# First stage of a gated attention and expert kernel: written-out orders, and the next stage's first weights and key rows loaded in it

## What is computed

```python
ek = jnp.exp(jnp.minimum(kf, 30.0)); ekv = ek * vf          # keys = values = the side input
a = a * decay + ekv_t; b = b * decay + ek_t                 # forward (nf, df), backward (nb, db)
euk = jnp.exp(jnp.minimum(u + kf, 30.0))
num = nf + nb - ekv + euk * vf
den = df + db - ek + euk
base = jax.nn.sigmoid(r) * (num / jnp.maximum(den, 1e-08))
...
q = (x @ Wq + bq).reshape(b, h, t, dh)
k = (x @ Wk + bk).reshape(b, t, h, dh).transpose(0, 2, 3, 1)
v = (x @ Wv + bv).reshape(b, t, h, dh).transpose(0, 2, 1, 3)
logits = jnp.einsum('bhtd,bhds->bhts', q, k) * scale
weights = jax.nn.softmax(logits + mask, axis=-1)
return out @ Wo + bo
```

## Time and profile before

| | us |
|---|---|
| runs of the kernel | 2507.57 median of 3 (2503.07 to 2509.45) |
| the profiled execution | 2524.23, its span 2522.4 |
| PE busy | 2255.8 (89%) |
| GpSimd busy | 1442.2 (57%) |
| VectorE busy | 1264.3 (50%) |
| ScalarE busy | 1165.6 (46%) |
| mean granted clock of TensorE | 0.95 of full |

### The profile page before, as it was taken

How to read it: one execution, slowest core, us unless ns; L and a number is a source line. 1 busy time by engine, 2 the same in 40 slices (tenths; PEclk the granted TensorE clock), 3 DMA queues, 4 the chain that set the end, 5 groups by cost and what they waited for, 6 DMA issues and landing times. The chain is left out here.

```text
span 2522.4 us, 42005 instructions
## 1 busy us (share of the span) xinstructions
PE 2255.8 (89%) x12059; PEld 1931.3 (77%) x12060; DVE 1264.3 (50%) x2118; ACT 1165.6 (46%) x2503; POOL 1442.2 (57%) x980
## 2 busy tenths in 40 slices
PE   1579999999999999898887989999999799999776
PEld 1458888888888878777776779999998699999654
DVE  6737777777765666757642322222222122222365
ACT  3347777777777767775621123333322133333210
POOL 7747777777755466565723036250659966430376
PEclk6789999999999999999978999999999899999887
DMA  4243444433364445443357045343547655442376
GB/s 121 71 131 113 126 126 131 159 120 114 116 214 126 145 160 178 158 162 133 134 200 276 5 133 181 112 156 98 182 147 221 199 186 179 148 164 77 117 205 179
DMA packets 285670, 372.37 MB, mean 148 GB/s; under 512 B 20212, under 2 KB 187192, under 8 KB 280824
## 3 DMA queue, kind: packets, MB, share of 16 engines
q1 hardware_dynamic: 229112, 251.41, 31.7%
q10 hardware_dynamic: 41088, 69.22, 8.3%
q0 software_dynamic: 15360, 50.34, 6.1%
HBM read 257.66 MB, written 113.25 MB: 147 GB/s over the span
## 5 line engine op out<-in xcount | busy, mean ns | idle before, releaser
L1933 POOL TENSOR_SCALAR we_high<-we_raw 128x1408 fp32r<-128x1408 f32 (+1 forms) x95 | 133.9, 1410 | 414.4 <-PE up_e L649 314.9
L1935 POOL TENSOR_TENSOR we_low<-we_raw,we_high 128x1408 fp32r<-128x1408 f32 (+1 forms) x95 | 314.6, 3311 | 7.9
L2064 DVE TENSOR_TENSOR hT_low<-hT_ps,hT_high 128x256 fp32r<-128x256 f32 x127 | 54.0, 425 | 391.4 <-ACT hT_high L2027 391.4
L2077 DVE TENSOR_TENSOR hidden_e<-silu_e,up_e 128x352 f32<-128x352 f32 x127 | 66.2, 521 | 282.6 <-ACT silu_e L2038 282.6
L2038 ACT ACTIVATE silu_e<-gate_e 128x352 f32<-128x352 f32 x127 | 59.0, 465 | 315.9 <-PE up_e L649 315.9
L649 PE MATMUL gate_e<-we_high,xT_high 128*128 x508 | 177.4, 349 | 21.1 <-POOL we_low L1935 20.7
L2043 ACT ACTIVATE rows_out<-down_e 128x512 f32<-128x512 f32 x127 | 75.9, 598 | 216.5 <-PE down_e L649 216.5
L649 PE MATMUL gate_e<-we_high,xT_low 128*128 x508 | 165.5, 326 | 0.0
L649 PE MATMUL gate_e<-we_low,xT_high 128*128 x508 | 165.2, 325 | 0.0
L649 PE MATMUL up_e<-we_high,xT_high 128*128 x508 | 164.0, 323 | 0.0
L649 PE MATMUL up_e<-we_high,xT_low 128*128 x508 | 163.0, 321 | 0.0
(11 more groups left out here) (341 smaller groups left out, 7337.5 us busy)
## 6 DMA issues: line engine op xcount, KB each, us to landing
rows_early<-slots_in ACTq DMA_DIRECT2D x129, 256.0 KB, 2.7
slots_out<-rows_out ACTq DMA_DIRECT2D x127, 256.0 KB, 2.1
we_raw<-L_ffn_w_gate SPq DMA_DIRECT2D x32, 704.0 KB, 4.6
we_raw<-L_ffn_w_up SPq DMA_DIRECT2D x32, 704.0 KB, 5.0
q_T<-q_out SPq DMA_DIRECT2D x64, 256.0 KB, 2.3
q_raw<-q_T SPq DMA_DIRECT2D x16, 1024.0 KB
w_ring<-L_attn_Wk SPq DMA_DIRECT2D x64, 256.0 KB
w_ring<-L_attn_Wv SPq DMA_DIRECT2D x64, 256.0 KB
```

Source lines behind the costliest of these rows:

```text
L1933: nc.gpsimd.tensor_scalar(wh[:, p, at:to], raw[:, at:to], 1.0, 1.0, ALU.mult, ALU.mult).then_inc(w_hi, 1)
L1935: nc.gpsimd.tensor_tensor(wl[:, p, at:to], raw[:, at:to], wh[:, p, at:to].bitcast(F32), ALU.subtract).then_inc(w_split, 1)
L2077: nc.vector.tensor_tensor(hb[:], sg[:], psu[:], ALU.mult).then_inc(h_done, 1)
```

## The change

The loops of the first stage's five engines are replaced by five lists (`FIRST_PE` and so on) that `turns` walks; a letter is a step, its number the chunk or the query group. GpSimd's `products` is cut in two (o and p). The key rows of batch 1 are issued from SP, behind the rows of x. The four-slot ring and the buffer of key rows are now allocated for both stages (`keep["w_ring"]`, `keep["k_rows"]`), and at the end of the first stage SP loads the second stage's first four units (n0 to n3: K of heads 0 and 1, two parts of V) and its first key rows (K0) into them. The second stage leaves these loads out. `store_xT` waits for the store before it. In full it reads (steps that only lose their loop are left out):

```diff
+FIRST_PE = (
+    "k0 v0 k1 x0 k2 x1 k3 k4 x2 k5 k6 x3 x4 k7 x5 Q0 Q1 Q2 Q3 Q4 x6 Q5 Q6 Q7 Q8 Q9 Q10 x7 Q11 Q12 Q13 Q14 Q15 "
+).split()
+FIRST_ACT = (
+    "t0 t1 E0 E1 h0 F0 t2 h1 E2 h2 h3 t3 c0 F1 h4 E3 t4 h5 c1 h6 F2 h7 F3 E4 F4 t5 h8 E5 c2 h9 c3 e0 t6 h10 e1 t7 "
+    "h11 E6 e2 F5 e3 e4 F6 e5 c4 E7 e6 e7 h12 e8 h13 e9 c5 h14 e10 e11 h15 F7 e12 c6 e13 e14 c7 e15 "
+).split()
+FIRST_DVE = (
+    "m0 m1 s0 s1 m2 f0 m3 l0 s2 f1 m4 l1 s3 f2 m5 f3 l2 l3 s4 m6 s5 f4 m7 s6 f5 l4 s7 f6 l5 f7 l6 l7 "
+).split()
+FIRST_POOL = (
+    "o0 p0 o1 p1 a0 a1 o2 q0 p2 q1 q2 o3 q3 a2 p3 q4 q5 a3 o4 q6 p4 q7 q8 o5 q9 p5 q10 a4 q11 o6 a5 p6 o7 p7 q12 "
+    "q13 a6 q14 a7 q15 "
+).split()
+FIRST_SP = (
+    "w4 w5 w6 w7 w8 w9 w10 O0 w11 O1 O2 w12 O3 X4 X5 w13 O4 w14 O5 O6 O7 O8 w15 O9 X6 O10 O11 K0 n0 O12 X7 n1 O13 "
+    "n2 O14 O15 n3 "
+).split()
+
+
+def turns(order, **steps):
+
+    for turn in order:
+        steps[turn[0]](int(turn[1:]))
...
-        qraw = sb("wq0_raw", [P, QR, S])
+        qraw = keep["w_ring"]
...
-            for j in range(QR, H):
-                load_wq(j)
+            sp.wait_ge(k_in[0], 16)
+            for n in range(KC, N):
+                sp.dma_start(kin[:, n, :, :], column(fs, n)).then_inc(k_in[0], 16)
+
+            def load_next(i):
+                sp.wait_ge(u_lo, H + i - RING + 1)
+                w, h, it = weight_stream()[i]
+                dst = qraw[:, (H + i) % QR, :]
...
+                sp.dma_start(dst, unit_source(wq, wk, wv, None, w, h, it)).then_inc(u_in[(H + i) % QR], 16)
+
+            def load_keys(n):
+                sp.dma_start(keep["k_rows"][:], column(fs, KC * 2 + n)).then_inc(keep["k_in"], 16)
 
             def store_xT(n):
                 sp.wait_ge(x_left, n - KC + 1)
+                if n > KC:
+                    sp.wait_ge(xt_out, 16 * (n - KC))
...
+            turns(FIRST_SP, w=load_wq, X=store_xT, O=store_q, n=load_next, K=load_keys)
...
-            def products(n):
+            def first_product(n):
...
+            def other_products(n):
...
+            turns(FIRST_POOL, o=first_product, p=other_products, q=low, a=sums)
...
+            turns(FIRST_PE, k=keys, v=vectors, x=rows_x, Q=queries)
...
-            keys(0)
+            order = list(FIRST_ACT)
+            turns(order[:1], t=keys)
...
-            exponentials(0)
-            act.wait_ge(k_in[0], 16)
-            for n in range(KC, N):
-                act.dma_start(kin[:, n, :, :], column(fs, n)).then_inc(k_in[0], 16)
...
+            turns(order[1:], t=keys, E=exponentials, h=high, F=factor, c=c_high, e=queries)
...
+            turns(FIRST_DVE[1:], m=minima, l=low, s=scans, f=fraction)
...
-SP_START = "lq u u u u Nx u u u U U U U".split()
+SP_START = "lq Nx u u u U U U U".split()
...
-        ring = sb("w_ring", [P, RING, S])
+        ring = keep["w_ring"]
...
-            load_k(1, 0)
             for it in range(-1, NIT):
-                units, ahead = iter(units_of(it)[0 if it < 0 else AHEAD:]), iter(units_of(it + 1))
+                units, ahead = iter(units_of(it)[RING if it < 0 else AHEAD:]), iter(units_of(it + 1))
...
+            keep["w_ring"], keep["k_rows"] = s2("w_ring", [P, RING, S]), s2("k_rows", [P, TC, P])
+            keep["k_in"] = two.enter_context(nc.semaphore("k_rows_in"))
```

More of the change, by code:

```diff
@@ L79, in chunk, with first_gates @@
     return tensor[:].rearrange("p b k s -> p (b k) s")[:, bass.ds(n, 1), :].rearrange("p o s -> p (o s)")
-def first_gates(nc, keep, dr, x, fs, cond, w1, u1, bq, bk, bv, bo, w2, u2, wq):
+FIRST_PE = (
[19 more added lines that the diff above has]
+        steps[turn[0]](int(turn[1:]))
+def first_gates(nc, keep, dr, x, fs, cond, w1, u1, bq, bk, bv, bo, w2, u2, wq, wk, wv):
     ident, cols, bqs, par1, par2, one = (keep[k] for k in ("ident", "cols", "bqs", "par1", "par2", "one"))
@@ L237, in queries, with vectors @@
                                                    for k in range(KC)], True, True).then_inc(q_mm, 1)
-            keys(0)
[L240 to L250, removed]
+            def vectors(n):
+                pe.wait_ge(v_in, 16 * (len(vec) + 1))
+                nc.tensor.transpose(psv, rows[:], ident[0:V_N, 0:V_N]).then_inc(x_T, 1)
+            turns(FIRST_PE, k=keys, v=vectors, x=rows_x, Q=queries)
         @block.scalar
@@ L501, in rows_of, with unit_source @@
     return u if u >= 0 else None
+def unit_source(wq, wk, wv, wo, w, h, it):
+    g = it % NG
+    at = (g * HG + h) * D
+    if w in "QK":
+        return (wq if w == "Q" else wk)[:, at:at + D].rearrange("(k p) m -> p k m", p=P)
+    if w == "V":
+        return wv[h * P:(h + 1) * P, g * HG * D:(g + 1) * HG * D]
+    return wo[at:at + D, :]
 def projections():
@@ L687, in attention @@
         c_out, c_in, acc_in = sem("c_stored"), sem("c_loaded"), sem("x1_loaded")
-        k_in, x_in, f_out, x1_out = sem("k_rows_in"), sem("x_rows_in"), sem("f2_stored"), sem("x1_stored")
+        k_in, x_in, f_out, x1_out = keep["k_in"], sem("x_rows_in"), sem("f2_stored"), sem("x1_stored")
         consts = sem("consts_done")
@@ L716, in attention @@
         gate_batch = lambda gate, it: it // NG + 2 if gate == 1 else it // NG
-        def w_source(w, h, it):
-            g = it % NG
-            at = (g * HG + h) * D
-            if w in "QK":
-                return (wq if w == "Q" else wk)[:, at:at + D].rearrange("(k p) m -> p k m", p=P)
-            if w == "V":
-                return wv[h * P:(h + 1) * P, g * HG * D:(g + 1) * HG * D]
-            return wo[at:at + D, :]
+        w_source = lambda w, h, it: unit_source(wq, wk, wv, wo, w, h, it)
         def w_split(w, h, it, part):
```

17 lines of the change are left out of this document (5 added, 12 removed).

## The result

| | before | changed |
|---|---|---|
| plain runs, median of 4 each | 2505.32 (2501.83 to 2509.45) | 2472.3 (2468.11 to 2473.05) |
| span of the profiled execution | 2522.4 | 2469.9 |

The ratio is 0.9864, with a 95% interval of 0.9843 to 0.9885; a second series on another chip gave 0.9855 (0.984 to 0.987). The changed kernel is 33 to 36 us faster (29 to 40 by the intervals). Forecast were 2471 and 36.9 us, a ratio of 0.985. The spans differ by 52.5 us. I therefore compare the two traces up to that load only.

A forecast was written before the change was run, and what follows sets the result against it. VectorE and GpSimd were taken to bound the head together, in alternation, with TensorE bounding most of the rest. Gains of 31.4 (order), 0 (SP's queue) and 5.5 (early loads) sum to 36.9 us: 2507.57 to 2471, range 2462 to 2483.

The forecast's parts named there:

- What bounds the head: First slices: VectorE (18.78 of 20 us) and GpSimd (19.35) bound the head together in alternation, TensorE working 3.88.
- Part 1: First stage's new order: query group 0 starts at 63.8, the stage ends at 110.7 instead of 142.16, -31.4 us.
- by 0.2 us at the closest: First stage: GpSimd's sums are ready before VectorE's fractions of batch 0 want them, tightest at 56.9 against 57.1.
- Three engines end within 1.3 us: First stage's end: TensorE's, VectorE's and GpSimd's paths finish within 1.3 us of each other at 110.7, none with reserve.
- Part 2: SP's queue: four key loads moved there from ScalarE's queue cost nothing, with some 14 us of cover.
- Part 3: Second stage's start: early loads let TensorE start K at 149.15 instead of 154.64, -5.5 us, bounds 0 and 7.
- The other chain: ScalarE at the second stage's start: key copy, minima, exponentials and splits done by 154.8; V2's load has 4 us.
- rival 2: Second stage's start: another wait ends last, early loads bring nothing, only 31.4 remains, 2476; sign ScalarE idle; chance 0.12.
- The sum: Whole kernel: 31.4 + 5.5 = 36.9 us, span 2522.4 to 2485.5, plain median 2507.57 to 2471.
- 1 (ScalarE holds the evictions): First stage: ScalarE's in-order waits stop query evictions three times, 14 us at worst, 9 with one absorbed; 2480; chance 0.20.
- 3 (lower level for all groups): First stage: TensorE never reaches its upper clock level among mixed queries and waits, net +24, 2531; chance 0.04.
- 4 (the loop gives it back): First iterations: early work only waits longer at the next meeting point, all but a few us returned, 2503; chance 0.04.

The follow-up runs named there:

- e4: The change with all 16 query groups behind TensorE's last transposes, their evictions and stores behind the other work; 2498.4 us, ratio 0.9969 to before.
- e0: The changed kernel run once more with nothing altered, on another chip; 2471.9 us, ratio 0.9855 to before.
- e1: The change with the early loads taken out, so only the first stage's new orders remain; 2474.9 us, ratio 0.9881 to before.
- e5: The change plus 30 useless TensorE products ahead of query group 0; 2472.7 us, ratio 0.9867 to before.
- e10: The change with batch 1's key rows issued from ScalarE's queue again, as before; 2472.1 us, ratio 0.9855 to before.
- e2: The change with the first stage's old orders, only the second stage's early loads kept; 2501.7 us, ratio 0.9983 to before.
- e9: The change with ScalarE splitting the first two K units before it waits for the gate weights' load; 2469.6 us, ratio 0.9856 to before.
- e6: The change plus useless TensorE products both at the second stage's start and ahead of query group 0; 2474.3 us, ratio 0.9866 to before.
- e11: The change plus 30 useless products before query group 0, three weights' low parts on VectorE, K split before the gate weights' wait; slower chip, ratio 0.9865.
- e3: The change plus useless TensorE products in four idle stretches of the second stage's start; 2475.9 us, ratio 0.9877 to before.

## Why the prediction was right, step by step

**What bounds the head.** Right. VectorE and GpSimd alternated there and TensorE waited; e4 shows that hiding TensorE's 46 us under them is the gain.

**Part 1, -31.4 forecast.** Measured -29.5 (142.16 to 112.64) and -30.2 in e0, with e1 29.8 us in time. The mechanism was right, the sum 1.9 short, and that by terms that cancel in part. Too small were: s0's start (16.46, not 15.6, as m1 took 2.65 instead of 1.99, both its minima beside GpSimd, rows 13.81 and 15.05), and the waits (7.0 us, not 3.7). The claim that a3 would be in time "by 0.2 us at the closest" failed: f3 waited 1.16, since GpSimd, from o0 to a3 without a stop, had instructions of up to 1.5 us. m6's wait was 2.07 instead of 1.5, as group 0 took 4.98 instead of 4.35, its products being 0.43 apart for longer. f4 waited 1.84 instead of 0.5. Too large was VectorE's work: 89.2 us from the first scan to the end, where the forecast has 90.1 and 1.3. The later pairs of minima took 1.71 to 1.84 and not 1.99, and m6's only 0.74. That these errors cancel so far is luck.

"Three engines end within 1.3 us" was not quite so: GpSimd's last instruction ended at 107.62, TensorE at 111.25, VectorE at 112.64, and the last eviction, at 112.49, came right behind c7. TensorE alone would have allowed 111.9. In e0 it was done at 110.04 and the stage ended at 112.00 all the same. VectorE, with its waits for GpSimd, was last each time with the new order except in e4, and that is why e5, which makes TensorE early, gave at most 0.7. "Errors lie on the late side" was right.

**Part 2, nothing.** Right (e10). Weight loads took 2.6 to 2.7 us from the issue to the split where ScalarE waited for them (34.95 to 37.66), against 2.3 assumed; VectorE did not notice.

**Part 3, -5.5 forecast.** K's first product moved from 9.72 to 4.45 behind the first load, the scores from 21.05 to 15.33: 5.3 and 5.7. e2 in time: 4.3 (1.5 to 6.8 by its interval). e9 shows that the wait named, for the gate weights, was the one before K. The other chain, through V2's load, was closer than the 4 us of cover suggest: ScalarE waited 0.61, 0.75 and 0.15 for V2, V3 and Q, the very sign given for rival 2, and only the 0.77 for the second K group kept it off the path.

**The sum.** 36.9 forecast; 33 by the medians of the first series, 34 and 36 by the ratios. By the places the change gives 35.3 at the scores (165.97 to 130.68), 1.6 less than forecast, which is Part 1's 1.9 less 0.2 that Part 3 gave more. That the absolute time, 2472.3, came within 2 us of the 2471 is in part luck: before's median was 2505.3 in the result, 2.3 under the one that the forecast started from.

**The rivals.** 1 (ScalarE holds the evictions): the fifteen groups show no stop in the trace; only the last eviction stood behind c7, for 0.6 us. 2 (the ring brings nothing): refuted by e2, whose scores came 6.0 us earlier, though its wait was near (Part 3). 3 (lower level for all groups): group 1 began at 0.23 apart, and no fall shows over 16 groups in two banks. The rule that the prediction cites from the Trainium skill ("TensorE: Matmul & The Clock Gate", section "A second HAM failure mode: psum-queue depth-cycling") is on short idles between groups; as the trace shows no idle between these, it is not put to the test. 4 (the loop gives it back): some 2 us of it were lost in iteration 0 in three of the thirteen profiled executions with new orders or early loads, 0.6 in one (e6), none in the other nine, e0 among them; from the second load of queries to the last the change took 980.2 us and before 979.4.

## What to carry to other kernels

Where two engines alternate at full load and a third waits for part of their results, write the order so that the third starts at its first complete input, and count each engine's own work from its own start: the largest of the three sums is the floor, and what lies between it and the end are the waits worth chasing. When the ends lie within some 2 us, taking one wait away gives little (0.7 us in e5, 1.5 in e11, nothing that the time shows); ask for each proposed cure which engine stands next, and whether the wait comes back as work: in e5 1.4 of 2.1 us did, as longer instructions, and e11 moved work onto the engine that was last. Here the part of the head that was gained was passed on whole by a loop that waits for semaphores alone. An apparent loss in one profiled execution should be looked for in a second one before it is explained.

## What the runs showed of the hardware

**The clock line can be blind at first.** In the changed kernel's trace the granted clock reads 1.00 for the whole first 113 us, yet group 0's products at 65.48 and 65.90 lie 0.43 us apart, the spacing at the 1.2 GHz level, and from 69.24 on 0.23. The traces of e0, e1, e3, e4, e6 and e9 have the same 9 in the first slice; those of before and of the other kernels a 6. The spacing of like matmuls is the safer sign.

**VectorE beside GpSimd.** A subtraction of two 128x512 SBUF operands on VectorE took 0.68 at 57.24 in e11, when GpSimd idled 1.57 us before its next step, and 1.78 at 71.79 beside its work. The Trainium skill, "SBUF — State Buffer", section "Who interferes with whom", says that a VectorE instruction with two SBUF inputs contends with a GpSimd instruction that reads SBUF; the 1.78 agrees. The scans, whose decay comes from PSUM, kept 1.2 us in both cases. The minima, with one 128x512 operand, took 0.43 and 0.48 when they started while GpSimd idled (at 70.88 and 71.22), and up to 1.6 beside it, but not always. One turn of the changed kernel, and what GpSimd ran beside it and beside the minimum at 15.05; then the same first minimum and GpSimd's sum in e11:

```profile
43.55 0.42 DVE L341 TENSOR_SCALAR g_ek<-g_kt 128x512 f32<-128x512 f32 x1
43.89 1.50 DVE L342 TENSOR_SCALAR g_eu<-g_kt,cols 128x512 f32<-128x512 f32 x1
...
14.81 1.45 POOL L219 TENSOR_TENSOR g_dl<-g_eu,g_ek 128x512 f32<-128x512 f32 x1
...
43.60 1.50 POOL L227 TENSOR_TENSOR g_db<-g_df,g_db 128x512 f32<-128x512 f32 x1
```

```profile
43.42 1.57 DVE L354 TENSOR_SCALAR g_ek<-g_kt 128x512 f32<-128x512 f32 x1
...
43.44 1.26 POOL L230 TENSOR_TENSOR g_db<-g_df,g_db 128x512 f32<-128x512 f32 x1
```

In the change the minimum at 43.55 took 0.42, and the sum that starts at 43.60 took 1.50 instead of 1.26. In e11, where the two start 0.02 us apart, it is the other way round: 1.57 and 1.26. So one of the two stands until the other is through, and a few hundredths of a us decide which. All seven minima of the change that took over 1 us end 0.28 or 0.29 us after the GpSimd instruction inside which they started (the one at 15.05 ends at 16.54, the product of 14.81 at 16.26). This is also a part of why the places of two executions differ: f2 starts at 50.38 in the change and at 51.39 in e11, whose lists are the same up to there.
